# Two cross-attention layers on one core: where TensorE's fill work, value products and VectorE's copies stand in a round

## The reference

```
layer 0 (32 query heads of 16, 8 key/value heads):
  q = x@Wq + bq;  k = ctx@Wk + bk;  v = ctx@Wv + bv
  attn = softmax(q k^T / 4 + mask);  y = (attn v)@Wo + bo + x
  x = (y - mean)/sqrt(var + 1e-6) * gamma + beta
layer 1 (16 heads of 32):
  a = layernorm(ctx);  Q = x@Wq^T;  K = a@Wk^T;  V = a@Wv^T
  out = softmax(Q K^T * 32**-0.5, masked) V
  x = x + tanh(gate) * (out@Wo^T)
```

## Time and profile before

| | us |
|---|---|
| median of the three timed runs | 1238.89 |
| the profiled execution | 1238.88 |
| its span | 1237.1 |
| PE busy / weight loads busy | 1163.7 / 942.3 |
| DVE busy / ACT busy / POOL busy | 810.3 / 749.9 / 259.9 |

### The profile page before, as it was taken

The page is one execution under the profiler, slowest core; times in us unless marked ns, Lnnn a source line. Parts: engine busy times, 40 slices in busy tenths (PEclk is TensorE's granted clock), DMA queues, the critical chain, the costliest instruction groups (busy, mean ns, idle before and its releaser), DMA issues.

```text
span 1237.1 us, 32215 instructions
## 1 busy us (share of the span) xinstructions
PE 1163.7 (94%) x9987; PEld 942.3 (76%) x9987; DVE 810.3 (65%) x2387; ACT 749.9 (61%) x2163; POOL 259.9 (21%) x280
## 2 busy tenths in 40 slices
PE   4899999999999999999999999999999999999997
PEld 4678787777878777787877778777787877778785
DVE  4465667667576775757667575766757576676734
ACT  3374756747475674747567474856747476574744
POOL 2042213121131312113121121312112131212210
PEclk9799999999999999999999999999999999999999
DMA  7674536447353654736365472635637263563600
GB/s 240 180 175 99 143 88 157 117 100 189 81 156 76 147 134 91 193 75 156 86 135 146 88 195 68 163 88 123 158 88 181 71 162 98 110 167 81 149 11 8
DMA packets 77821, 153.77 MB, mean 124 GB/s; under 512 B 10384, under 2 KB 47056, under 8 KB 77152
## 3 DMA queue, kind: packets, MB, share of 16 engines
q1 hardware_dynamic: 77792, 153.40, 50.6%
HBM read 113.72 MB, written 39.65 MB: 124 GB/s over the span
## 4 chain that ended last, share of the span: by engine, by line
PE 72%; issue 12%; DVE 9%; ACT 4%; DMA 1%; DVEq 1%; POOL 1%; ACTq 0%; SPq 0%; POOLq 0%
PE PJ L365 17%; PE TP L416 13%; PE SCO L402 6%; PE OA L436 5%; PE SCO L460 5%; PE SCO L681 5%; PE PJ L378 5%; PE PJ L468 4%; DVE SCO L819 3%; PE SCO L406 3%; PE SCO L365 2%; ACT PR L1049 2%; DVE PT L829 2%; DVE MN L819 1%; PE SCO L666 1%
## 5 line engine op out<-in xcount | busy, mean ns | idle before, releaser
L1049 ACT ACTIVATE PR<-SCO,MN 100x361 f32<-100x361 f32 x768 | 424.8, 564 | 154.3 <-DVE MN L819 151.1
L819 DVE CUSTOM_DVE_ANT_0 SCO<-SCO,MK 100x361 f32<-100x361 f32 x768 | 402.3, 549 | 148.1 <-PE SCO L402 102.3
L416 PE MATMUL TP<-ident,PR 100*128 100x100 f32 x2304 | 268.4, 252 | 22.3 <-DVE PT L829 19.7
L416 PEld LDWEIGHTS TP<-ident,PR 100*128 100x128 f32 x2304 | 226.9, 141 | 80.5 <-DVE PT L829 27.1
L1060 ACT ACTIVATE PT<-TP 121x600 f32<-121x600 f32 x256 | 173.0, 676 | 77.0 <-PE TP L416 76.6
L402 PE MATMUL SCO<-K0S,Q0S 128*100 128x362 f32 x512 | 164.1, 375 | 19.7 <-ACT PR L1049 17.5
L1049 ACT ACTIVATION_READ_ACCUMULATOR PR<-SCO,MN 100x1 f32 x768 | 158.2, 206 | 0.0
L829 DVE COPY PT<-TP 121x600 f32<-121x600 f32 x128 | 100.0, 781 | 52.1 <-PE TP L416 50.1
L819 DVE DVE_READ_ACCUMULATOR2_ANT MN<- 100x1 f32 x768 | 108.7, 141 | 0.0
L402 PEld LDWEIGHTS SCO<-K0S,Q0S 128*100 128x100 f32 x512 | 75.4, 166 | 43.1 <-ACT PR L1049 38.2
L406 PE MATMUL SCO<-K1S,Q1S 128*100 128x362 f32 x256 | 96.6, 387 | 8.1 <-ACT Q1S L1171 5.0
(11 more groups left out here) (142 smaller groups left out, 1827.7 us busy)
## 6 DMA issues: line engine op xcount, KB each, us to landing
K1S<-k_scr SPq DMA_DIRECT2D x128, 364.0 KB, 6.1
k_scr<-K1HL SPq DMA_DIRECT2D x64, 364.0 KB, 2.5
Q0S<-q_scr SPq DMA_DIRECT2D x128, 100.0 KB, 3.9
K0S<-k_scr SPq DMA_DIRECT2D x64, 182.0 KB, 4.8
AT<-ctx_cols SPq DMA_DIRECT2D x16, 722.0 KB, 9.3
V<-ctx_rows SPq DMA_DIRECT2D x16, 484.0 KB
q_scr<-QHL SPq DMA_DIRECT2D x16, 400.0 KB, 2.5
k_scr<-K1HL SPq DMA_DIRECT2D x32, 182.0 KB, 3.1
```

What stands on the lines that cost most here:

```text
L416: last = pe.transpose(TP[:, k % 2, c * T:(c + 1) * T], PR[0:T, k % NPR, c * SP:c * SP + P], ident[0:T, 0:T])
L819: dve.tensor_tensor_reduce(out=bank, in0=bank, in1=mask[0:T, :], scale=scale, scalar=3.4e38, op0=ALU.add, op1=ALU.min, accum_out=MN[0:T, k ...
L1049: act.activation(PR[0:T, k % NPR, 0:S], SCO[0:T, k % 3, 0:S], ACT.Exp, bias=MN[0:T, k:k + 1], scale=-1.0, accum_out=SM[0:T, k:k + 1]).then ...
```

## The change

In layer 0 the two scores of a round no longer stand together. The fill work of the round is cut in two by `halved`: the first half (rounded up) stands between head 2p and head 2p+1, the second behind head 2p+1. The value products of rounds 4 and 9 also stand between the two scores; those of round 12 stand behind both, with the fill step ahead of head 25. The product of h = 2 moves from ahead of the next batch's queries to behind them. The 12 K1 steps of rounds 0 to 2 are 4, 4, 4 where they were 2, 5, 5.

In layer 1, VectorE's copies in rounds 20 and 22 stand ahead of the row maxima of both heads (they stood between them). REP_BANK swaps two banks, and the first scores wait for the copies of Q1S one by one. All six parts of h = 4 stand in round 23, where two stood; the other four stood in round 0 of the next batch.

```
-        K1_LATE = spans({0: 2, 1: 5, 2: 5})
+        K1_LATE = spans({0: 4, 1: 4, 2: 4})
-        PV0_PARTS = {9: (0, 0, 3), 12: (1, 0, 3)}
-        PV1_TAIL = {0: (4, 2, 6), 4: (5, 0, 6)}
-        REP_BANK = (SCO[:, 2, 0:C * T], TP[:, 0, 0:C * T], TP[:, 1, 0:C * T], SCO[:, 0, 0:C * T])
+        REP_BANK = (SCO[:, 2, 0:C * T], SCO[:, 0, 0:C * T], TP[:, 1, 0:C * T], TP[:, 0, 0:C * T])
...
+            def halved(span, part):
+                at = (span[0] + span[1] + 1) // 2
+                return range(span[0], at) if part == 0 else range(at, span[1])
...
-                    for k in (2 * p, 2 * p + 1):
-                        if k >= 3 or not first:
-                            pe.wait_ge(prob, NH * b + k - 2)
-                        score(b, k)
-                    if p in PV1_TAIL and not first:
-                        h, i, j = PV1_TAIL[p]
-                        out_half(b - 1, h, range(i, j))
-                    if p in PV0_PARTS:
-                        h, i, j = PV0_PARTS[p]
-                        out_half(b, h, range(i, j))
-                        if p == 12:
-                            sums_transposed(b, 0)
+                    if p >= 2 or not first:
+                        pe.wait_ge(prob, NH * b + 2 * p - 2)
+                    score(b, 2 * p)
+                    if first:
+                        first_keys1_steps(p, 0)
+                    else:
+                        keys1_steps(b, p, 0)
+                    values1_steps(b, first, p, 0)
+                    if p in OUT1_STEPS and not first:
+                        if p == 7:
+                            pe.wait_ge(attn, 3 * b)
+                        out1(b - 1, halved(OUT1_STEPS[p], 0))
+                    if p == 4 and not first:
+                        out_half(b - 1, 5, range(6))
+                    elif p == 9:
+                        out_half(b, 0, range(3))
+                    if p >= 1 or not first:
+                        pe.wait_ge(prob, NH * b + 2 * p - 1)
+                    score(b, 2 * p + 1)
+                    if p == 12:
+                        out_half(b, 1, range(3))
+                        sums_transposed(b, 0)
...
-                out_half(b, 2, range(3))
                 if more:
                     pe.wait_ge(l_xt, 16 * b + 32)
...
+                out_half(b, 2, range(3))
                 out_half(b, 3, range(3))
...
                     if p == 16:
+                        pe.wait_ge(rep_act, 2 * b + 1)
+                        pe.wait_ge(k1ld[0], 64 * b + 64)
+                    elif p == 17:
                         pe.wait_ge(rep_act, 2 * b + 2)
-                        pe.wait_ge(rep_dve, 2 * b + 2)
-                        pe.wait_ge(k1ld[0], 64 * b + 64)
...
+                    if p == 16:
+                        pe.wait_ge(rep_dve, 2 * b + 1)
+                    elif p == 17:
+                        pe.wait_ge(rep_dve, 2 * b + 2)
...
-                        out_half(b, 4, range(2))
+                        out_half(b, 4, range(6))
...
-            out_half(NB - 1, 4, range(2, 6))
...
-                    shift(b, 2 * p)
                     if p in (20, 22):
                         probs_out(b, p - 3)
-                    elif more and p == 18:
+                    shift(b, 2 * p)
+                    if more and p == 18:
```

More of the change, by code:

```diff
@@ L541, in values1_means, with first_keys1_steps @@
                 last.then_inc(wv_cm, 1)
-            def first_keys1_steps(p):
-                for i in range(*FIRST_K1_STEPS.get(p, (0, 0))):
+            def halved(span, part):
+                at = (span[0] + span[1] + 1) // 2
+                return range(span[0], at) if part == 0 else range(at, span[1])
+            def first_keys1_steps(p, part):
+                for i in halved(FIRST_K1_STEPS.get(p, (0, 0)), part):
                     if i == 0:
@@ L553, in first_keys1_steps, with keys1_steps @@
                     keys1(0, i)
-            def keys1_steps(b, p):
-                for i in range(*K1_STEPS.get(p, (0, 0))):
+            def keys1_steps(b, p, part):
+                for i in halved(K1_STEPS.get(p, (0, 0)), part):
                     if i == 9 * C:
@@ L559, in keys1_steps, with values1_steps @@
                     keys1(b, i)
-            def values1_steps(b, first, p):
-                for i in range(*(FIRST_V1_STEPS if first else V1_STEPS).get(p, (0, 0))):
+            def values1_steps(b, first, p, part):
+                for i in halved((FIRST_V1_STEPS if first else V1_STEPS).get(p, (0, 0)), part):
                     if i == 0:
@@ L601, in batch @@
                     if first:
-                        first_keys1_steps(p)
+                        first_keys1_steps(p, 1)
                     else:
-                        keys1_steps(b, p)
-                    values1_steps(b, first, p)
+                        keys1_steps(b, p, 1)
+                    values1_steps(b, first, p, 1)
                     if first and p == 0:
@@ L615, in batch @@
                     if p in OUT1_STEPS and not first:
-                        if p == 7:
-                            pe.wait_ge(attn, 3 * b)
-                        out1(b - 1, range(*OUT1_STEPS[p]))
+                        out1(b - 1, halved(OUT1_STEPS[p], 1))
                     if p >= 2:
```

## The result

The changed kernel takes 1243.63 us (median of five runs, 1243.49 to 1244.49); the kernel before took 1238.76 beside it (1238.04 to 1239.21). The ratio is 1.0040, with a 95% interval of 1.0029 to 1.0051: slower by 4.9 us. The profiled execution after took 1243.49, its span 1241.7, which is 4.6 more than before. The granted clock was 0.991 of full speed in the profiled execution before and 0.992 in the one after, so the clock has no part in the difference.

The account below looks back on a forecast made before the run. It took chains handed between TensorE, VectorE and ScalarE, not TensorE alone, as the bound. Fourteen looped batches at +0.59 gave +8.3; with -2.2, +1.5 and -1.1, +6.5 on 1238.88: 1245 us, range 1225 to 1254.

Parts of the forecast that it names:

- a string of VectorE that decides from head 19 on: Rounds 9 to 12: head 19's later score delays VectorE's maximum, result and following work; V1 step 12 waits 1.0 us.
- layer 1 (up to head 0): End of layer 1: earlier copies and Q1S waits win, grouped products cost some back; -0.66 us a batch.
- rounds 0 to 7: Early layer 0: ScalarE-VectorE chain decides, out1 only 0.6 to 0.7 earlier, head 15 +0.2; batch 0.44 ahead after round 7.
- rounds 9 to 12: Layer 0: head 19 behind 24 value products delays VectorE's work and V1 step 12; head 26 later, +0.57 us.
- rounds 13 to 15: End of layer 0: later head 27 delays exponential 29, pair 12's copy and pair 13's transposes; +0.46 us.
- between the layers: Middle of the batch: h=2 product only changes place, 1.15 us either way, nothing waits for earlier queries; zero.
- rival 2: Whole kernel: TensorE is the bound throughout, all score waits come back, -3.0 us a batch, 1193 us; chance 0.06.
- The split's own price: Layer 0's split rounds: between nothing and 0.08 us a round, 0 to 1.2 a batch; nothing taken.
- Rival 1: Behind head 19: VectorE's string does not decide; -0.44 to -1.0 us a batch, 1221 to 1230 us; chance 0.20.
- Rival 3: Round 10: new wait paid in full, later waits absorb nothing; +1.1 us a batch, 1252 up to 1258; chance 0.14.
- Rival 4: Whole kernel: gains of layer 1 and losses of round 10 cancel, 1239 us; chance 0.10.
- First and last batch: Outside the loop: first -1.5 for filled waits and -0.66 for layer 1; last +1.5 and -1.1 us.

Follow-up runs that it names:

- e1: Kernel before with only the layer 1 part of the change, layer 0 keeping both scores together: 1226.97 us, ratio 0.9910.
- e7: e6 with head 15's score again ahead of out1's wait for VectorE's OT, out1's four steps of round 7 together behind it: 1220.79 us, ratio 0.9852.
- e12: e7 with the split in rounds 0 to 6 only, fill work of rounds 7 to 15 behind both scores: 1226.02 us, ratio 0.9903.
- e3: Changed kernel with the value products of round 9 put back behind head 19's score: 1228.22 us, ratio 0.9916.
- e4: Changed kernel with rounds 13 to 15 not split, all V1 steps behind both scores: 1238.79 us, ratio 1.0004.
- e11: Changed kernel with the product of h = 2 ahead of the next batch's queries again: 1244.97 us, ratio 1.0059.
- e5: e1 without the grouping: two parts of h = 4 in round 23, four in round 0, K1 steps 2, 5, 5: 1216.28 us, ratio 0.9816.
- e10: Kernel before with only VectorE's copies in rounds 20 and 22 moved ahead of both row maxima: 1221.24 us, ratio 0.9864.
- e8: Changed kernel with VectorE's result behind head 18's row maximum instead of head 19's, TensorE's order unchanged: 1233.71 us, ratio 0.9960.
- e6: Changed kernel with the edits of e3 and e4 together: 1223.58 us, ratio 0.9875.
- e2: Changed kernel with its layer 1 part undone, leaving only layer 0's part: 1255.46 us, ratio 1.0136.

## Why the prediction was right, and where its sizes were off

The forecast, 1245 with a string of VectorE that decides from head 19 on, holds: 1243.6, slower, and by the mechanism that was named. Point by point, in us of a looped batch against before (negative is earlier), each term with the drift between two marks of the traces, medians over the 14 looped batches. The marks are layer 1's queries, head 0, head 18, head 26, pair 13's transposes and the queries again:

| term | forecast | trace | experiment |
|---|---|---|---|
| layer 1 (up to head 0) | -0.66 | -0.75 | e1: -0.75 |
| rounds 0 to 7 | +0.22 | +0.13 | e7: 0.12 for head 15; e12: nothing for the split of 0 to 6 |
| rounds 9 to 12 | +0.57 | +0.75 | e3: 1.01 for round 9, -0.27 for the rest (e7 against e12: -0.26) |
| rounds 13 to 15 | +0.46 | +0.32 | e4: 0.33 |
| between the layers | 0 | -0.10 | e11: -0.12 |
| sum | +0.59 | +0.35 | mean pace +0.35 |

**Layer 1.** Head 47 was to come 1.31 earlier and came 1.51 earlier, both counted from the layer-1 queries that TensorE makes in the middle; pair 21's transposes 0.62, measured 0.74; 1.9 from head 47 to the next head 0, measured 2.02. The grouping was charged 0.69 there (1.17 for 0.48) and gives nothing back in round 0. e5 shows both: 0.57 in layer 1, and nothing won in layer 0. The copies (e10, 1.12) and Q1S (0.28) were each a little better than the walk of heads 40 to 47 had them.

**Rounds 0 to 7.** The claim that ScalarE and VectorE keep the lead was the step that argued against rival 2, and it is the best supported one: head 3's wait grew from 0.29 to 0.49, `out1` starts right behind a wait for OT, and e12 against e1 shows layer 0 unchanged to 0.01 us. Two sizes were off: head 3 waits 0.49 for a forecast 0.7, and head 15 behind `out1`'s wait costs 0.12 for 0.2. Rival 2 (1193) is refuted: in e1 the scores wait 47.9 us for ScalarE, 9.7 more than before, and the kernel is faster, so the total of a wait is not what can be won. The Trainium skill, "Perfetto Trace Analysis", section "Identifying Performance Opportunities", starts from the engine with the highest occupancy, but it does not take the matmul busy share for a measure of how near TensorE is to its limit, and it would have the dependencies that end the gaps start sooner or complete faster. The runs bear that out: filling TensorE's gaps of rounds 0 to 6 with other work moved them and brought nothing (e12 against e1, where TensorE's rows cover 95%), and two copies that start sooner brought 1.12 us a batch (e10). So the page speaks for rival 2 less than the prediction had it.

**Rounds 9 to 12.** The steps came out as walked: head 19's maximum T+2.07 (forecast 2.0), `result` 2.53 (2.5), V1 step 12 3.33 (3.41), head 20's maximum 4.28 (4.25), head 22's 6.41 (6.38), head 25 7.89 (7.83). Only the last link was mis-sized. From head 25 to head 26 the sum had 2.07, the trace has 2.18: the products start 0.34 behind a score that itself had waited, not 0.25. That 0.11 and the 0.06 by which head 25 is late make T+10.07 out of T+9.9, which is all that the term is short. Rival 1 (the string does not decide, 1226) is refuted by e3 and most plainly by e8: moving only `result` on VectorE, with TensorE's order left alone, brings 0.66 a batch. Rival 3 (the wait paid in full, 1252 and more) charged 1.1 for round 9, and e3 measures 1.01, so its price for that one edit was near, and it was right that no later wait absorbs it. But the splits of rounds 10 to 12 give 0.27 back. Rival 1 had named the waits of the old order that would go (0.2 each in rounds 11, 12 and 15), though not this sum. Neither rival 3 nor the forecast had it as a term of its own; the forecast's T+9.9 for head 26 is the two together. Rival 4 (gains and losses cancel, 1239) is refuted by the time: every run of the kernel after is longer than every run of the kernel before beside it.

**Rounds 13 to 15.** 0.46 was forecast, 0.32 came. The mechanism (ScalarE's pair 12 copy late, TensorE waiting for it) shows in the row at 605.67. Head 27 stands 0.93 behind head 26, as forecast (0.94). From head 27 to pair 13's transposes the forecast's own figures leave 4.76 us and the trace has 4.64; which step of that string is 0.12 shorter is open. It is not that round 9's lateness was charged a second time: e3 and e6 differ by the same 0.32 with round 9's wait gone. Pair 13's transposes were forecast at T+15.6 and stand at T+15.64, because the 0.17 missing up to head 26 and the 0.13 too much behind it nearly cancel.

**Between the layers** zero was taken and 0.10 won. The step that failed is "1.15 us either way": behind the queries the product of h = 2 stands together with that of h = 3, and the two take 2.17 for 2.30 (e11).

**The split's own price**, 0 to 0.08 a round with 0 taken: in e12 seven split rounds cost nothing that shows (0.00 in layer 0). That fits both zero and a price hidden by the waits, so the bound stays for rounds in which TensorE does not wait.

**First and last batch.** For the first batch -2.2 was forecast (-1.5 for the fill work and -0.66 for layer 1) and -0.8 came. This is the term furthest off. The account of the profiled execution is 0.1 at the start, -0.83 for the first batch, 14 x 0.35 for the loop, 0.25 and 0.18 for the last batch and the tail: +4.6. The step that failed is that filling the first batch's waits, such as head 7's, would bring something: from head 4 to head 9 the first batch takes 7.78 us before and after, although head 7's wait fell from 1.60 to 0.92. That is the chain of rounds 0 to 7 again. From head 4 to the end the first batch is 0.28 longer after than before (78.94 for 78.66), and of the 0.66 credited for layer 1 only 0.10 is there, counted from pair 13's transposes. The 0.83 by which it is shorter lies ahead of head 4 (9.48 from head 0, for 10.59). That stretch varies by itself: the first batches of e6 and e7 are written alike and take 11.01 and 9.70 there, and 78.75 and 78.82 behind it. So nothing of the 0.83 can be put down to the change. The last batch and tail were put at +0.4 in sum (+1.5 and -1.1) and gave +0.43.

The forecast's 1245 is near for a second reason as well: the loop was charged 3.4 us too much (0.59 for 0.35, fourteen times), and the first batch was credited with 1.4 too much. One error covered part of the other, and inside the loop's sum four terms were too high by 0.42 together and rounds 9 to 12 too low by 0.18. That the time came within 2 us is in part luck; the direction and the place of the loss are not.

## What to carry to other kernels

When three engines hand a short chain round, walk that chain with start-to-start steps before moving anything: where the chain through the others is the longer one, filling the gaps of the busiest engine brings nothing and shows as waits that move to the next link (rounds 0 to 6 here). Where a score waits and the chain behind it has room, the same filling wins (0.26 us a batch in rounds 8 and 10 to 12). Before an instruction is pushed back by a microsecond, list what stands behind its consumer on the in-order engine: one score that came 1 us late carried `result` and all of VectorE's work behind it along, made a new wait on TensorE, and cost 1.0 us a batch. Test the parts of a combined change by themselves: here one part (two copies ahead of a row maximum each) was worth 17 us alone, and four others more than ate it up: the value products of round 9 (1.01 us a batch), the grouping (0.65), the late splits (0.33) and head 15 (0.12).

## What the runs showed that I had not expected

The parts were additive within 0.05 us a batch (e1 + e2, e3 + e4, e7 + e5), although each of them worked through waits. I had expected gains of one place to vanish in the waits of the next; they did so in rounds 0 to 6 only, where TensorE waited for heads 3, 7 and 11 already. And the grouping of 48 value products, which takes no more TensorE time than 16 and 32 (48 in 1.17 us, from the starts of the rows; 16 in 0.48 and 32 in 0.82), cost 0.65 us a batch purely by its place.
